# A sequence layer with a spectral feed-forward part on one core: M centred as it is formed, normalisation factors taken for two tiles at once

## Time and profile before

| | us |
|---|---|
| median of 3 runs (982.04 to 982.98) | 982.52 |
| span of the profiled execution | 980.0 |
| of it, first pass and recurrence, up to the first residual of the second pass | about 530 |
| PE busy / DVE / ACT / POOL | 929.7 / 755.7 / 561.1 / 518.4 |

### The profile page before, as it was taken

How to read it: one execution, slowest core, us unless ns; L and a number is a source line. 1 busy time by engine, 2 the same in 40 slices (tenths; PEclk the granted TensorE clock), 3 DMA queues, 4 the chain that set the end, 5 groups by cost and what they waited for, 6 DMA issues and landing times.

```text
span 980.0 us, 19706 instructions
## 1 busy us (share of the span) xinstructions
PE 929.7 (95%) x5742; PEld 516.0 (53%) x5742; DVE 755.7 (77%) x1616; ACT 561.1 (57%) x1047; POOL 518.4 (53%) x1317
## 2 busy tenths in 40 slices
PE   5899999999999999996998999999999999999996
PEld 2455555555555555553776555545545455454543
DVE  5598878888788787875668788787787877878774
ACT  2243333333333333343465588878888888888887
POOL 0152222222222222216114888889888898888984
PEclk9889999999999999997999999999999999999999
DMA  9144445554445554441603467676666676666753
GB/s 322 44 147 147 144 164 171 171 164 137 154 144 171 171 171 153 145 151 40 241 2 82 165 226 240 227 232 239 227 228 230 227 244 220 232 233 224 247 172 129
DMA packets 89483, 175.84 MB, mean 179 GB/s; under 512 B 3057, under 2 KB 5361, under 8 KB 89458
## 3 DMA queue, kind: packets, MB, share of 16 engines
q1 hardware_dynamic: 85856, 170.80, 51.9%
q10 hardware_dynamic: 3602, 4.74, 1.5%
HBM read 106.45 MB, written 67.11 MB: 177 GB/s over the span
## 4 chain that ended last, share of the span: by engine, by line
PE 47%; POOL 33%; issue 11%; DVE 4%; ACT 2%; ACTq 1%; DMA 1%; POOLq 1%; DVEq 0%
POOL x_sb L689 12%; PE bank L1164 11%; PE bank L1165 11%; PE bank L1167 11%; POOL rstd L635 7%; PE bank L1154 6%; POOL rnorm L713 4%; POOL scaled_mean L696 2%; POOL veps L633 2%; PE bank L1209 2%; POOL lift_bias L699 1%; PE bank L1188 1%; POOL rstd L715 1%; POOL nbias L717 1%; ACTq L437 1%
## 5 line engine op out<-in xcount | busy, mean ns | idle before, releaser
L926 DVE SCALAR_TENSOR_TENSOR lo_sb<-bank,hi_sb 128x512 f16<-128x512 f32 x256 | 176.7, 690 | 93.8 <-ACT hi_sb L444 73.0
L444 ACT ACTIVATE hi_sb<-bank 128x512 f16<-128x512 f32 x128 | 76.4, 597 | 291.4 <-PE bank L1154 280.6
L633 POOL TENSOR_TENSOR veps<-mv,c_eps 128x1 f32<-128x1 f32 x256 | 49.4, 193 | 311.3 <-DVE mv L907 296.3
L1164 PE MATMUL bank<-z_sb,hi_sb 128*128 128x512 f16 x512 | 194.2, 379 | 9.1 <-DVE w_ring L1098 7.9
L1164 PE MATMUL bank<-wg_hi,hi_sb 128*128 128x512 f16 x512 | 197.7, 386 | 4.6 <-DVE wg_lo L794 3.8
L1165 PE MATMUL bank<-wg_lo,hi_sb 128*128 128x512 f16 x512 | 197.8, 386 | 0.0
L1165 PE MATMUL bank<-z_sb,hi_sb 128*128 128x512 f16 x512 | 194.2, 379 | 0.0
L1154 PE MATMUL bank<-cst,norm_sb 128*128 128x128 f32 x1024 | 160.6, 280 | 24.8 <-DVE norm_sb L920 23.0
L689 POOL TENSOR_TENSOR x_sb<-x_sb,gate_sb 128x512 f32<-128x512 f32 x128 | 163.4, 1277 | 11.8 <-DVE gate_sb L1086 11.3
L635 POOL TENSOR_TENSOR rstd<-veps,c_half 128x1 f32<-128x1 f32 x256 | 139.8, 546 | 20.1
L1154 PEld LDWEIGHTS bank<-cst,norm_sb 128*128 128x128 f32 x1024 | 119.2, 142 | 51.1 <-DVE norm_sb L920 15.0
(11 more groups left out here) (157 smaller groups left out, 1220.5 us busy)
## 6 DMA issues: line engine op xcount, KB each, us to landing
x_sb<-x SPq DMA_DIRECT2D x63, 1024.0 KB, 6.2
gate_dram<-gate_sb SPq DMA_DIRECT2D x32, 1024.0 KB, 5.3
gate_sb<-gate_dram SPq DMA_DIRECT2D x32, 1024.0 KB, 5.3
out<-out_sb SPq DMA_DIRECT2D x31, 1024.0 KB, 5.3
h_rep<-fourier_constants ACTq DMA_DIRECT2D x2, 514.0 KB, 14.8
x_sb<-x SPq DMA_DIRECT2D x2, 512.0 KB, 6.5
w_ring<-w_gate SPq DMA_DIRECT2D x2, 512.0 KB, 6.3
w_re_sb<-w_freq_real ACTq DMA_DIRECT2D x1, 1024.0 KB, 11.5
```

The source lines that it names most:

```text
L926: nc.vector.scalar_tensor_tensor(lo_sb[:, k % 2].rearrange("p t r -> p (t r)"), ps_t[k % 2][:], ROW_SCALE, hi_sb[:, k % 2].rearrange("p t ...
L1164: nc.tensor.matmul(dst, hi_sb[:, k % 2, t], w_hi[:, t], start=(t == 0), stop=False)
```

## The change

In words: (1) `combine` sums the rows of M as it writes them (two accumulator outputs), waits for its own result, and forms from the two sums minus the mean of the row (`m_shift`); ACT adds this when it takes the high half, DVE when it takes the low half. Every row of u @ M then has mean 0, so u @ M + u has the mean 1/8, a constant. The scale bound of M is doubled. (2) `ffn_sum` gives no row sum any more, `minus_mean` is gone, `squares` waits for the sum directly and has a constant bias and a scale 1/sqrt(512), and `scale_and_bias` has three instructions in place of four. (3) `rstd_of` and `lifted_bias`, once a slot, become `normalise_factors`, once in every odd slot, for the tiles n+3 and n+4; its wait is for the aggregate of tile n+4.

```diff
@@ act
             def high_m(i):
-                act.wait_ge(s_pair, 2 * KT + i + 1)
-                nc.scalar.activation(m_hi[:, i], m_sb[:, i], ACT.Copy).then_inc(s_m_hi, 1)
+                act.wait_ge(s_mshift, i + 1)
+                nc.scalar.activation(m_hi[:, i], m_sb[:, i], ACT.Identity,
+                                     bias=m_shift[:, i:i + 1]).then_inc(s_m_hi, 1)
...
-            def b_normalise(n, k):
-                act.wait_ge(s_blift, n + 1)
+            def b_normalise(n, k, v):
+                act.wait_ge(s_blift, v * 4 + k // 2 + 1)
...
             def squares(n, k):
-                act.wait_ge(s_negmu, n + 1)
+                act.wait_ge(s_w, n + 1)
...
-                nc.scalar.activation(gsum_sb[:, k % 2], w_ring[:, k], ACT.Square, bias=negmu[:, k:k + 1],
+                nc.scalar.activation(gsum_sb[:, k % 2], w_ring[:, k], ACT.Square, bias=c_squares[:],
+                                     scale=1.0 / float(np.sqrt(D)),
                                      accum_out=vsum[:, k:k + 1]).then_inc(s_sq, 1)
@@ pool
-            def lifted_bias(n, k):
-
-                c = slice(k % 4, k % 4 + 1)
-                pool.wait_ge(s_brstd, n + 1)
-                pool.tensor_tensor(scaled_mean[:, c], mv[:, k % 4, 0:1], rstd[:, c],
-                                   ALU.mult).then_inc(s_bmr, 1)
-                pool.wait_ge(s_bmr, n + 1)
+            def normalise_factors(m, k):
+
+                c = slice(k % 4, k % 4 + 2)
+                pool.wait_ge(s_baggr, m * 2 + 2)
+                pool.tensor_tensor(veps[:, c], mv[:, c, 1], c_eps4[:], ALU.add).then_inc(s_bveps, 1)
+                pool.wait_ge(s_bveps, m + 1)
+                pool.tensor_tensor(rstd[:, c], veps[:, c], c_half[:], ALU.pow).then_inc(s_brstd, 1)
+                pool.wait_ge(s_brstd, m + 1)
+                pool.tensor_tensor(scaled_mean[:, c], mv[:, c, 0], rstd[:, c], ALU.mult).then_inc(s_bmr, 1)
+                pool.wait_ge(s_bmr, m + 1)
                 pool.tensor_tensor(lift_bias[:, c], c_lift[:], scaled_mean[:, c],
                                    ALU.subtract).then_inc(s_blift, 1)
 
-            def minus_mean(n, k):
-                pool.wait_ge(s_w, n + 1)
-                pool.tensor_tensor(negmu[:, k:k + 1], wsum[:, k:k + 1], c_mean[:],
-                                   ALU.mult).then_inc(s_negmu, 1)
-
             def scale_and_bias(m, k):
...
-                pool.tensor_tensor(rnorm2[:, c], var2[:, c], c_half[:], ALU.pow).then_inc(s_rnorm2, 1)
-                pool.wait_ge(s_rnorm2, m + 1)
-                pool.tensor_tensor(rstd2[:, c], rnorm2[:, c], c_rootd[:], ALU.mult).then_inc(s_rstd2, 1)
+                pool.tensor_tensor(rstd2[:, c], var2[:, c], c_half[:], ALU.pow).then_inc(s_rstd2, 1)
                 pool.wait_ge(s_rstd2, m + 1)
-                pool.tensor_tensor(nbias2[:, c], negmu[:, c], rstd2[:, c], ALU.mult).then_inc(s_nb2, 1)
+                pool.tensor_tensor(nbias2[:, c], c_neglift[:], rstd2[:, c], ALU.mult).then_inc(s_nb2, 1)
 
             def slot(n, k, v):
-                if exists(n + 3):
-                    rstd_of(n + 3, (k + 3) % 8, s_baggr, s_bveps, s_brstd, c_eps4)
-                    lifted_bias(n + 3, (k + 3) % 8)
-                if exists(n - 2):
-                    minus_mean(n - 2, (k - 2) % 8)
+                if k % 2 == 1 and exists(n + 3):
+                    normalise_factors(v * 4 + (k + 3) // 2, (k + 3) % 8)
                 if exists(n + 5):
                     residual(n + 5, (k + 5) % 8, v if k < 3 else v + 1)
                 if k % 2 == 0 and exists(n - 4):
                     scale_and_bias(v * 4 + k // 2 - 2, (k - 4) % 8)
@@ dve
+                wait_own(nc.vector.tensor_scalar(bias_max[:], bias_max[:], 2.0, None, ALU.mult))
...
+                else:
+                    sums = m_sums[:, q - 2 * KT]
+                    nc.vector.scalar_tensor_tensor(dst[:, 0:HALF], odd[:, 0:HALF], ratio[sign], even, ALU.mult,
+                                                   ALU.add, accum_out=sums[:, 0:1])
+                    wait_own(nc.vector.scalar_tensor_tensor(
+                        dst[:, HALF:D], odd[:, HALF - 2:0:-1], ratio[-sign], even[:, HALF - 2:0:-1], ALU.mult,
+                        ALU.add, accum_out=sums[:, 1:2]))
+                    nc.vector.sem_inc(done, 1)
+                    nc.vector.tensor_scalar(m_shift[:, q - 2 * KT:q - 2 * KT + 1], sums[:, 0:1], sums[:, 1:2],
+                                            -1.0 / D, ALU.add, ALU.mult).then_inc(s_mshift, 1)
...
             def low_m(i):
                 dve.wait_ge(s_m_hi, i + 1)
-                nc.vector.tensor_tensor(m_lo[:, i], m_sb[:, i], m_hi[:, i],
-                                        ALU.subtract).then_inc(s_msplit, 1)
+                nc.vector.scalar_tensor_tensor(m_lo[:, i], m_sb[:, i], m_shift[:, i:i + 1], m_hi[:, i], ALU.add,
+                                               ALU.subtract).then_inc(s_msplit, 1)
...
                 nc.vector.scalar_tensor_tensor(w_ring[:, k], ps_g[k % 2][:], unscale[:, 3:4],
-                                               norm_sb[:, k % 4], ALU.mult, ALU.add,
-                                               accum_out=wsum[:, k:k + 1]).then_inc(s_w, 1)
+                                               norm_sb[:, k % 4], ALU.mult, ALU.add).then_inc(s_w, 1)
```

More of the change, by code:

```diff
@@ L171, in build @@
         lift_bias = sb("lift_bias", [P, 4])
-        c_lift = sb("c_lift", [P, 1])
+        c_lift = sb("c_lift", [P, 2])
         c_eps = sb("c_eps", [P, 1])
-        c_eps4 = sb("c_eps4", [P, 1])
+        c_eps4 = sb("c_eps4", [P, 2])
         c_half = sb("c_half", [P, 2])
-        wsum = sb("wsum", [P, 8])
-        negmu = sb("negmu", [P, 8])
+        m_sums = sb("m_sums", [P, KT, 2])
+        m_shift = sb("m_shift", [P, KT])
+        c_neglift = sb("c_neglift", [P, 2])
+        c_squares = sb("c_squares", [P, 1])
         vsum = sb("vsum", [P, 8])
         var2 = sb("var2", [P, 8])
-        rnorm2 = sb("rnorm2", [P, 8])
         rstd2 = sb("rstd2", [P, 8])
-        c_mean = sb("c_mean", [P, 1])
-        c_epsd = sb("c_epsd", [P, 2])
-        c_rootd = sb("c_rootd", [P, 2])
+        c_eps2 = sb("c_eps2", [P, 2])
         nbias2 = sb("nbias2", [P, 8])
@@ L265, in build @@
         s_msplit = sem("m_split")
+        s_mshift = sem("m_centred")
         s_high = sem("scan_high_half")
@@ L609, in slot @@
                 if exists(n + 2):
-                    b_normalise(n + 2, (k + 2) % 8)
+                    b_normalise(n + 2, (k + 2) % 8, v if k < 6 else v + 1)
                 if exists(n - 5) and not (isinstance(n, int) and n - 5 == TILES - 1):
@@ L621, in _ @@
             pool.memset(c_eps4[:], LN_EPS / 4)
-            pool.memset(c_mean[:], -1.0 / D)
+            pool.memset(c_neglift[:], -LIFT)
+            pool.memset(c_squares[:], -LIFT / float(np.sqrt(D)))
             pool.memset(c_lift[:], LIFT)
-            pool.memset(c_epsd[:], LN_EPS * D)
-            pool.memset(c_rootd[:], float(np.sqrt(D)))
+            pool.memset(c_eps2[:], LN_EPS)
             pool.memset(c_half[:], -0.5).then_inc(s_pool_const, 1)
@@ L710, in scale_and_bias @@
                 pool.wait_ge(s_sq, m * 2 + 2)
-                pool.tensor_tensor(var2[:, c], vsum[:, c], c_epsd[:], ALU.add).then_inc(s_var2, 1)
+                pool.tensor_tensor(var2[:, c], vsum[:, c], c_eps2[:], ALU.add).then_inc(s_var2, 1)
                 pool.wait_ge(s_var2, m + 1)
-                pool.tensor_tensor(rnorm2[:, c], var2[:, c], c_half[:], ALU.pow).then_inc(s_rnorm2, 1)
-                pool.wait_ge(s_rnorm2, m + 1)
-                pool.tensor_tensor(rstd2[:, c], rnorm2[:, c], c_rootd[:], ALU.mult).then_inc(s_rstd2, 1)
+                pool.tensor_tensor(rstd2[:, c], var2[:, c], c_half[:], ALU.pow).then_inc(s_rstd2, 1)
                 pool.wait_ge(s_rstd2, m + 1)
-                pool.tensor_tensor(nbias2[:, c], negmu[:, c], rstd2[:, c], ALU.mult).then_inc(s_nb2, 1)
+                pool.tensor_tensor(nbias2[:, c], c_neglift[:], rstd2[:, c], ALU.mult).then_inc(s_nb2, 1)
             def slot(n, k, v):
-                if exists(n + 3):
-                    rstd_of(n + 3, (k + 3) % 8, s_baggr, s_bveps, s_brstd, c_eps4)
-                    lifted_bias(n + 3, (k + 3) % 8)
-                if exists(n - 2):
-                    minus_mean(n - 2, (k - 2) % 8)
+                if k % 2 == 1 and exists(n + 3):
+                    normalise_factors(v * 4 + (k + 3) // 2, (k + 3) % 8)
                 if exists(n + 5):
@@ L879, in scale_of_m @@
             def scale_of_m():
-                wait_own(nc.vector.scalar_tensor_tensor(amax_all[:, 3:4], w_abs_all[:], 2.0 / D, bias_max[:],
+                wait_own(nc.vector.scalar_tensor_tensor(amax_all[:, 3:4], w_abs_all[:], 4.0 / D, bias_max[:],
                                                         ALU.mult, ALU.add))
@@ L1007, in combine @@
                     ratio = {1: 1.0 / WAVE_SCALE, -1: -1.0 / WAVE_SCALE}
[L1008 to L1011, removed]
```

(10 more changed lines are left out.)

2 lines of the change are left out of this document (removed).

## The result

The changed kernel took 1008.13 us (median of 4 runs, 1005.75 to 1009.70) against 982.28 before: a ratio of 1.0265, with a 95% interval of 1.0246 to 1.0283. The forecast was 1009. Its profiled execution has a span of 1005.8 us and took 1007.57.

What follows compares the result with a forecast made beforehand. POOL was taken to bound the second pass at 6.82 us a pair. The new pair loop's +24.3 and the start's +2.0, the end nothing, on 982.5 gave 1008.8, about 1009 us; range 994 to 1019.

Steps and rivals of the forecast that it cites:

- The bound before: Second pass of the kernel before: POOL sets the pace at 6.82 us a pair of tiles; PE's floor is 6.48.
- POOL's work after: Second pass: POOL's own work falls from 6.82 to 5.15 us a pair.
- The loop, step by step: POOL's wait for the second tile's aggregate closes a five-step loop through DVE: 7.17 us a pair, bounds 7.03 to 7.29.
- The long stretch: Aggregate of tile 3 to that of tile 127: 62 pairs at 7.17 us, 444.5 less 420.2, +24.3 us.
- The accumulator read that I took at 0.03: DVE's removed read after the sum tile, in statistics to statistics: saves 0 to 0.08 us a pair, taken as 0.03.
- The timetable: Engine times within a pair after the aggregate: other waits have half a microsecond or more in hand, so none stretches the loop.
- the sign that PE would wait for the sum once a pair: Second pass: PE waits for DVE's sum once a pair, 0.5 us or so.
- The start: Before the aggregate of tile 3: one longer `combine` (0.4) and the pair's wait delay the statistics of tile 2, +2.0 us.
- The end: Last aggregate to last sum: 13.2 us against 12.65, +0.55; last chain 0.54 shorter; together nothing.
- PE as the bound: Rival for the second pass: only busy times count, a pair takes PE's 6.48 us, total 965 us; chance 0.08.
- The loop and the gain: Rival: loop of 6.78 to 6.82 us, POOL's saved time becomes idle, run stays near 983 us; chance 0.04.
- The clock: Rival: PE's longer idle times lower its clock; in a tenth of the second pass +31, 1040 us; chance 0.04.

Runs made afterwards that it cites:

- M centred alone: Changed kernel with the factors taken again once a slot for one tile; row-centred M and shorter second normalisation stay: 965.46 us, ratio 0.9822.
- Experiments 1 and 4: Changed kernel, residual of n+5 put before the pair of factors: 965.99 us; changed kernel, factors taken in even slots for n+2 and n+3: 966.29 us.
- experiment 3: Changed kernel plus a small POOL instruction: between pair's wait and factors 1024.63 us; at head of `scale_and_bias` 1007.58; the former with residual first 970.59.
- pairs alone: Kernel before with the factors taken in pairs and nothing else of the change; row sums and minus mean stay: 1014.85 us, ratio 1.0328.
- the residual first alone: Kernel before with the residual moved ahead of the one-tile factors and nothing else: 997.07 us, ratio 1.0137.

## Why the prediction was right

- **The bound before.** Right: POOL's work set the pace. M centred alone, which takes 0.57 us of small instructions off POOL's pair (6.82 to 6.25), gives 965.5, PE's pace.
- **POOL's work after.** Forecast 5.15 us a pair, of 7.13: 72%. The window shows 67.0 of 100 us of busy records, without the gaps of 0.07 between small instructions; a pair of 7.13 less POOL's wait of 1.97 is 5.16. Right.
- **The loop, step by step** (forecast, measured in the pair shown above): aggregate to factor 0.25, 0.25; factors to residual 1.48, 1.50 and 1.46; residual to statistics 1.31, 1.30; statistics to statistics 2.73 to 2.82, 2.72; statistics to aggregate 1.34 to 1.43, 1.33. Sum 7.17, 7.10; over 62 pairs 7.13, because in some pairs, like the one of 7.25, the low half starts 0.82 and not 0.72 after the statistics. Why it does is open. Experiments 1 and 4 open the loop and the time goes; experiment 3 lengthens it and 62 x 0.27 = 16.7 us come, 16.5 measured; outside it the same instruction costs nothing. The cause is shown.
- **The long stretch.** +24.3 forecast, +22.1 measured: the pair was 0.04 too long. The accumulator read that I took at 0.03 was worth nothing: the statistics start 706.62 - 705.96 = 0.66 after the sum with or without it.
- **The timetable.** The forecast put PE's second product of the pair at 5.8 us after the aggregate's end, released by DVE's sum at 5.75, with ACT's high half ready at 5.5. It started at 706.85, 5.83 after, but the high half came at 5.80 and the sum at 5.68, so that the high half mostly released it. So the sign that PE would wait for the sum once a pair did not come. DVE's low half, at 707.34, took the high half with 0.5 us to spare where the forecast had 0.9, so the loop stayed alone. From 600 to 900 us, and in the pair shown:

```profile
PE bank L1168 <- ACT hi_sb L579: 8.6, 32, 0.3
PE bank L1168 <- DVE w_ring L1103: 3.0, 11, 0.3
...
706.85 0.38 PE L1168 MATMUL bank<-z_sb,hi_sb 128*128 128x512 f16 x1 [0.27 <-ACT hi_sb L579]
```

- **The start.** +2.0 forecast, +3.8 measured. From the first `combine` after the recurrence to the aggregate of tile 3 it is 2.3 us longer (543.19 - 529.17 = 14.0 against 539.43 - 527.71 = 11.7), near the forecast 2.0. Of its parts the pair's wait was right: from the end of the aggregate of tile 1 to the statistics of tile 2 it takes 2.89, for 0.08 + 1.48 + 1.31 = 2.87. M centred was costed too low: the aggregate of tile 1 is 1.0 later from that `combine`, where 0.4 was forecast, because two of the longer `combine` stand before it and the forecast counted one. With M centred alone this stretch is 1.5 longer, with pairs alone 1.3, so the two overlap in part. The other 1.5 us lie before it: 1.2 of them before the last `combine` beside the recurrence, where nothing of the second pass runs. That point lay between 524.3 and 526.8 us in the profiles of this study, also in kernels without M centred (525.7 with the residual first alone), so I read it as the first pass's own scatter and not as the change's; that is not tested.
- **The end.** 13.2 us forecast from the last aggregate to the last sum, 998.83 - 985.71 = 13.1 measured, and the last chain 0.55 shorter. Right.
- **The total.** 26.3 forecast, 25.8 measured. That it is right to 1 us is partly luck: the long stretch came 2.2 shorter and the start 1.8 longer than forecast, and most of the latter I read as scatter.
- **The rivals.** PE as the bound at 965 us: the price was right to a microsecond, and that kernel is one swap away; what failed is its condition. The loop and the gain did not cancel: 7.13 lies over 6.82. The clock did not fall in the long stretch: 1.00 from 560 to 1000 us although PE idled some 0.3 us in places each pair. The Trainium skill, TensorE: Matmul & The Clock Gate, section A second HAM failure mode: psum-queue depth-cycling, tells of a kernel whose clock swung with such short idle times; on gaps of 0.27 us the trace doesn't bear it out. At the start of the second pass it did stay low for longer. The same 4 us, first in the kernel before and then in the changed one:

```profile
543.00:547.00 4.00, 4.00 (x22) 2.10 (x21) 1.88 (x5) 1.29 (x2) 2.99 (x7) 1.00 0.00 0
543.00:547.00 4.00, 3.60 (x11) 1.29 (x10) 2.38 (x6) 1.41 (x2) 3.32 (x6) 0.50 0.64 238
```

PE had idled 0.80 and 1.70 us shortly before it fell in the changed kernel, 1.13 and 0.74 in the one before. The first pair after the aggregate of tile 3 took 7.82 us, against 7.21 before and 7.13 on average, so what the lower clock cost there is under 1 us.
- **What the prediction missed** cost it nothing, but the experiments much: the minus mean is a second chain through the same POOL queue (ACT's squares, then the high half). It was in the earlier trace rows as ACT's wait of 27.1 us, and I read it as a sign of POOL's load only.

## What to carry to other kernels

When an instruction is moved or batched so that its wait is for a later event, write down what is queued behind the wait on that engine, and follow it through the other engines' lists until it comes back: if it does, the loop's sum divided by the slots it spans is a pace of its own, and an engine that idles 2 us a pair can still be on it. The cure is not less work but the place: here a swap of two calls was worth 42 us, a wait one slot older the same, and one 0.19 us instruction in front of the wait instead of behind it 38 us. That last figure holds where the residual already stood ahead of the wait; with the residual still behind it, moving the same instruction gave 7.8 us. Each chain that runs through the wait has to be taken out before the time of the next one shows. Put what feeds other engines ahead of a wait, and what only that engine's own later work needs behind it.

## What the runs showed of the hardware that I had not expected

- POOL's power of -1/2 on two columns took 0.69 to 0.71 us and on one column 0.54; the additions and products took 0.19 and 0.20 either way, 0.27 from start to start with a wait on the one before. So four instructions for a pair take 1.46 to 1.50, and for a single tile 1.29 (707.50 to the minus mean's start).
- An accumulator output on DVE's 128 x 512 sum didn't delay the next instruction at all: it started 0.66 us after the sum in either kernel.
- The instruction behind DVE's statistics waits for them, and it started 0.72 to 0.82 us after them, against 0.61 to 0.67 behind its other instructions, for which it does not wait, all of 0.69 to 0.75 us by their records. The Trainium skill, VectorE: DVE Perf Modes, section The DRAIN you can't avoid, has such a wait at no extra cost; here it is some 0.1 us, and the measurement decides. (The statistics are the only ones of this size with such a wait here, so their kind may have a part in it. The prediction took the 0.82 against 0.73 as the evidence, but both of these stand behind the wait.) In the same way the new small instruction behind `combine` started after an idle 0.16 to 0.17 us, released by DVE itself.
